# Last stage of an attention kernel: TensorE products on 64-column halves, and keys, queries and layer norm tokens transposed in pieces of 64 rows

## The reference

```
for l in range(2):                       # DEPTH
    h = shift_token(x)                   # second half of the features comes from the token before
    q, k, v = split(h @ wqkv[l])         # 8 heads of 64
    q = l2norm(q) * q_scale; k = l2norm(k) * k_scale
    q, k = rotary_xpos(q, k)
    o = local_attention(q, k, v)         # windows of 128 tokens, each sees itself and the one before
    x = x + o @ wo[l]
    h = layernorm(shift_token(x)) * ln_g + ln_b
    a, g = split(h @ w1[l] + b1[l])      # 682 hidden columns each
    x = x + (a * gelu(g)) @ w2[l] + b2[l]
```

## Time and profile before

| | |
|---|---|
| median of 3 runs | 2962.0 us (2961.99 to 2963.34) |
| span of the profiled execution | 2960.1 us |
| instructions on TensorE | 38016 matmuls, 38016 weight loads |
| TensorE, VectorE, ScalarE, GpSimd busy | 99%, 79%, 77%, 38% of the span |

### The profile page before, as it was taken

How to read it: one execution, slowest core, us unless ns; L and a number is a source line. 1 busy time by engine, 2 the same in 40 slices (tenths; PEclk the granted TensorE clock), 3 DMA queues, 4 the chain that set the end, 5 groups by cost and what they waited for, 6 DMA issues and landing times.

```text
span 2960.1 us, 97183 instructions
## 1 busy us (share of the span) xinstructions
PE 2919.8 (99%) x38016; PEld 1971.1 (67%) x38016; DVE 2325.1 (79%) x4219; ACT 2271.1 (77%) x4379; POOL 1111.0 (38%) x1835
## 2 busy tenths in 40 slices
PE   8999999999999999999989999999999999999998
PEld 4455555555555555555567777778777777877786
DVE  8888888888888888888856776667676667767665
ACT  4599999999999999999956666666666666666664
POOL 5421221111112211221245455555456554555554
PEclk9899999999999999999999999999999999999999
DMA  6631111111111111111121101111011111011110
GB/s 231 212 116 38 49 47 45 40 49 48 43 44 49 49 41 46 49 49 38 43 64 44 32 30 33 40 43 40 28 36 30 44 43 34 28 35 38 44 41 5
DMA packets 157206, 152.14 MB, mean 51 GB/s; under 512 B 17794, under 2 KB 130946, under 8 KB 156930
## 3 DMA queue, kind: packets, MB, share of 16 engines
q1 hardware_dynamic: 156930, 148.15, 16.0%
HBM read 89.37 MB, written 58.72 MB: 50 GB/s over the span
## 4 chain that ended last, share of the span: by engine, by line
PE 95%; DVE 3%; issue 1%; ACT 1%; SPq 0%; DMA 0%; POOL 0%; DVEq 0%; POOLq 0%; ACTq 0%
PE banks L1488 15%; PE banks L1450 15%; PE banks L1505 15%; PE banks L1690 11%; PE banks L1555 8%; PE banks L1703 6%; PE banks L1606 4%; PE banks L1645 4%; PE banks L1657 4%; PE banks L1566 4%; PE banks L1622 2%; PE banks L1578 1%; PE banks L1632 1%; PE banks L1587 1%; PE banks L1713 1%
## 5 line engine op out<-in xcount | busy, mean ns | idle before, releaser
L1146 DVE TENSOR_REDUCE pair_max<-banks 128x1 f32<-128x1024 f32 x1024 | 1219.7, 1222 | 145.5 <-PE banks L1450 115.8
L917 ACT ACTIVATE probs<-banks 128x512 f32<-128x512 f32 x2048 | 1158.7, 598 | 64.0 <-PE banks L1488 4.1
L1488 PE MATMUL banks<-q_aug,k_aug 98*32 98x512 bf16 x8192 | 1143.6, 381 | 0.8 <-ACT probs L917 0.4
L1450 PE MATMUL banks<-k_aug,q_aug 96*32 96x512 bf16 x8192 | 819.4, 382 | 5.3 <-ACT v_all L884 3.3
L1505 PE MATMUL banks<-probs,v_cur 128*32 128x256 f32 x8192 | 796.8, 379 | 0.2
L1488 PEld LDWEIGHTS banks<-q_aug,k_aug 98*32 98x32 bf16 x8192 | 391.7, 95 | 197.1 <-ACT probs L917 5.4
L1505 PEld LDWEIGHTS banks<-probs,v_cur 128*32 128x32 f32 x8192 | 366.8, 111 | 166.5 <-ACT acc_sb L898 0.8
L646 POOL TENSOR_SCALAR row_max<-pair_max 128x1 f32<-128x1 f32 x508 | 132.1, 283 | 886.5 <-DVE pair_max L1146 886.5
L1450 PEld LDWEIGHTS banks<-k_aug,q_aug 96*32 96x32 bf16 x8192 | 310.1, 97 | 218.2 <-DVE pair_max L1146 11.6
L1690 PEld LDWEIGHTS banks<-hnT,w_sb 128*128 128x128 f32 (+1 forms) x2816 | 320.2, 191 | 25.1 <-ACT hnT L997 25.1
L1690 PE MATMUL banks<-hnT,w_sb 128*128 128x128 f32 (+1 forms) x2816 | 332.4, 278 | 0.9 <-ACT hnT L997 0.9
(11 more groups left out here) (146 smaller groups left out, 4093.4 us busy)
## 6 DMA issues: line engine op xcount, KB each, us to landing
acc_scratch<-acc_sb SPq DMA_DIRECT2D x128, 256.0 KB, 2.4
heads_win<-acc_scratch SPq DMA_DIRECT2D x512, 64.0 KB
q_aug<-q_parts SPq DMA_DIRECT2D x192, 64.0 KB, 2.2
k_aug<-k_parts SPq DMA_DIRECT2D x192, 64.0 KB, 2.2
q_parts<-parts SPq DMA_DIRECT2D x16, 384.0 KB, 3.1
k_parts<-parts SPq DMA_DIRECT2D x16, 384.0 KB, 4.0
x_in<-in_x SPq DMA_DIRECT2D x10, 512.0 KB, 4.7
xT_scratch<-xnT SPq DMA_DIRECT2D x8, 512.0 KB, 5.2
```

Of the source, the lines that this page charges most:

```text
L917: nc.scalar.activation(probs[:, step % PRING, :], banks[:, ring(h, use), :], ACT.Exp, scale=SCALE).then_inc(prob_ready, 1)
L1146: nc.vector.tensor_reduce(pair_max[:, group % 2, q, half:half + 1], banks[:, 4 + 2 * (t % 2):6 + 2 * (t % 2), :], AX.XY, ALU.max).then_inc ...
L1450: last = nc.tensor.matmul(banks[m:m + CT, 4 + t % 4, :], q_aug[0:TERM_ROWS, b, q * P + m:q * P + m + CT], k_aug[0:TERM_ROWS, b, kq * BANK: ...
L1488: last = nc.tensor.matmul(banks[m:m + CT, ring(h, use), :], k_aug[0:AUG, b, kb * P + m:kb * P + m + CT], q_aug[0:AUG, b, qc * CHUNK:(qc + ...
```

## The change

Four things are changed, all in the last stage.

1. Products on halves. A helper `in_halves` issues each product as two, on columns 0 to 63 and 64 to 127 of its weights. It is used for the query projection (`project` with n = 0), the value projection, `project_o`, `hidden`, `project_hidden` and `project_heads`. The key projection (n = 1) stays whole, and so do L1632 (row sums) and L1722 (`transpose_y`).
2. Transposes in pieces. A helper `turn_rows` transposes rows 0 to 63 of a tile into bank 1 and rows 64 to 127 into bank 2. Keys and queries are transposed by it in one function, `transpose_qk`, with one semaphore `qkT_done`, and x1T by it in `transpose_h`. Keys lie in the first 256 columns of the two banks, queries in the last 256.
3. Readers follow. `keep_k`, `keep_q` and `normalise` read across two banks. `keep_k` waits for `qkT_done`, which comes after the queries too. The values go to bank 3 instead of bank 2, and the waits on `sum_ready` and `y_kept` are exchanged accordingly.
4. Two semaphores that no engine waits for, `turns_seen` and `x1_seen`, are incremented by TensorE after its waits on `k_turned`, `q_turned` and `x1_ready`.

```diff
+            def in_halves(out, stationary, moving, start, stop):
+
+                cols = stationary.shape[-1]
+                for first in range(0, cols, COLS):
+                    size = min(COLS, cols - first)
+                    last = nc.tensor.matmul(out[first:first + size], stationary[:, first:first + size], moving,
+                                            start=start, stop=stop)
+                return last
...
-                    last = nc.tensor.matmul(banks[:, lanes(b) + n, :], xT[:, l, b, f, 1 - f:1 - f + WINDOW],
-                                            wqkv_sb[:, l, f, n * INNER:(n + 1) * INNER],
-                                            start=(f == 0), stop=(f == 1))
+                    out, tokens = banks[:, lanes(b) + n, :], xT[:, l, b, f, 1 - f:1 - f + WINDOW]
+                    weights = wqkv_sb[:, l, f, n * INNER:(n + 1) * INNER]
+                    if n == 1:
+                        last = nc.tensor.matmul(out, tokens, weights, start=(f == 0), stop=(f == 1))
+                    else:
+                        last = in_halves(out, tokens, weights, start=(f == 0), stop=(f == 1))
...
+            def turn_rows(b, at_col, tile):
+
+                for r in range(2):
+                    rows = slice(r * LD, (r + 1) * LD)
+                    last = nc.tensor.transpose(banks[:, lanes(b) + 1 + r, at_col:at_col + LD],
+                                               tile[rows], ident[rows, rows])
+                return last
+
+            def transpose_qk(i, k):
 
                 l, b = parts_of(k)
                 if l == 0:
                     pe.wait_ge(y_kept, final_of(i, k) + (B * (k // ITEMS) + 1))
...
+                pe.wait_ge(k_turned, at(i, k))
+                nc.tensor.sem_inc(turns_seen, 1)
+                for j in range(NPAIR):
+                    turn_rows(b, j * LD, turned[:, b, 1, j * P:(j + 1) * P])
                 for j in range(NPAIR):
                     if j % 2 == 0:
                         pe.wait_ge(q_turned, at(i, k, j // 2 + 1, 2))
-                    last = nc.tensor.transpose(banks[:, lanes(b) + 3, j * P:(j + 1) * P],
-                                               turned[:, b, 0, j * P:(j + 1) * P], ident[:])
-                last.then_inc(qT_done, 1)
...
+                        nc.tensor.sem_inc(turns_seen, 1)
+                    last = turn_rows(b, D + j * LD, turned[:, b, 0, j * P:(j + 1) * P])
+                last.then_inc(qkT_done, 1)
...
                 pe.wait_ge(x1_ready, at(i, k))
+                nc.tensor.sem_inc(x1_seen, 1)
                 for f in range(2):
-                    last = nc.tensor.transpose(banks[:, lanes(b) + 3, f * P:(f + 1) * P],
-                                               x1T[:, l, b, f, 1 - f:1 - f + WINDOW], ident[:])
+                    last = turn_rows(b, f * LD, x1T[:, l, b, f, 1 - f:1 - f + WINDOW])
                 last.then_inc(h_done, 1)
...
-                        last = nc.tensor.matmul(
-                            banks[0:width, lanes(b) + bank, place_ * P:(place_ + 1) * P],
-                            w1_sb[:, l, f, c * P:c * P + width], hnT[:, b, f, :], start=(f == 0), stop=(f == 1))
+                        last = in_halves(banks[0:width, lanes(b) + bank, place_ * P:(place_ + 1) * P],
+                                         w1_sb[:, l, f, c * P:c * P + width], hnT[:, b, f, :],
+                                         start=(f == 0), stop=(f == 1))
```

More of the change, by code:

```diff
@@ L280, in build @@
         k_turned = sem("k_turned")
-        qT_done = sem("qT_done")
-        kT_done = sem("kT_done")
+        qkT_done = sem("qkT_done")
+        turns_seen = sem("turns_seen")
+        x1_seen = sem("x1_seen")
         qT_kept = sem("qT_kept")
@@ L1295, in normalise @@
                 b = k % B
-                h_tok = banks[:, lanes(b) + 3, 0:D]
+                h_tok = banks[:, lanes(b) + 1:lanes(b) + 3, 0:P]
                 dve.wait_ge(h_done, at(i, k))
@@ L1563, in project_v @@
                 if l == 0:
-                    pe.wait_ge(y_kept, final_of(i, k) + (B * (k // ITEMS) + 1))
+                    pe.wait_ge(sum_ready, final_of(i, k) + (B * (k // ITEMS) + 1))
                 for f in range(2):
-                    last = nc.tensor.matmul(banks[:, lanes(b) + 2, :], xT[:, l, b, f, 1 - f:1 - f + WINDOW],
-                                            wqkv_sb[:, l, f, 2 * INNER:], start=(f == 0), stop=(f == 1))
+                    last = in_halves(banks[:, lanes(b) + 3, :], xT[:, l, b, f, 1 - f:1 - f + WINDOW],
+                                     wqkv_sb[:, l, f, 2 * INNER:], start=(f == 0), stop=(f == 1))
                 last.then_inc(v_ready, 1)
-            def transpose_q(i, k):
+            def turn_rows(b, at_col, tile):
[5 more added lines that the diff above has]
+            def transpose_qk(i, k):
                 l, b = parts_of(k)
                 if l == 0:
-                    pe.wait_ge(sum_ready, final_of(i, k) + (B * (k // ITEMS) + 1))
+                    pe.wait_ge(y_kept, final_of(i, k) + (B * (k // ITEMS) + 1))
+                pe.wait_ge(k_turned, at(i, k))
+                nc.tensor.sem_inc(turns_seen, 1)
+                for j in range(NPAIR):
+                    turn_rows(b, j * LD, turned[:, b, 1, j * P:(j + 1) * P])
                 for j in range(NPAIR):
@@ L1656, in project_o @@
                     for j in range(NPAIR):
-                        last = nc.tensor.matmul(banks[:, lanes(b) + 1, f * P:(f + 1) * P],
-                                                wo_sb[:, l, j, f * P:(f + 1) * P], oT[:, b, j, :],
-                                                start=(j == 0), stop=(j == NPAIR - 1))
+                        last = in_halves(banks[:, lanes(b) + 1, f * P:(f + 1) * P],
+                                         wo_sb[:, l, j, f * P:(f + 1) * P], oT[:, b, j, :],
+                                         start=(j == 0), stop=(j == NPAIR - 1))
                 last.then_inc(wo_done, 1)
@@ L1702, in project_hidden @@
                     for f in range(2):
-                        last = nc.tensor.matmul(banks[:, lanes(b), f * P:(f + 1) * P],
-                                                w2_sb[:, l, j, f * P:(f + 1) * P], uT[:, b, j, :],
-                                                start=(j == 0 and f == 0), stop=(j == HB - 1 and f == 1))
+                        last = in_halves(banks[:, lanes(b), f * P:(f + 1) * P],
+                                         w2_sb[:, l, j, f * P:(f + 1) * P], uT[:, b, j, :],
+                                         start=(j == 0 and f == 0), stop=(j == HB - 1 and f == 1))
                 last.then_inc(w2_done, 1)
@@ L1712, in project_heads @@
                 for f in range(2):
-                    last = nc.tensor.matmul(banks[:, lanes(b) + 3, 0:D], heads_T[:, b, f, :], wp_sb[:, f, :],
-                                            start=(f == 0), stop=(f == 1))
+                    last = in_halves(banks[:, lanes(b) + 3, 0:D], heads_T[:, b, f, :], wp_sb[:, f, :],
+                                     start=(f == 0), stop=(f == 1))
                 last.then_inc(proj_done, 1)
```

34 lines of the change are left out of this document (15 added, 19 removed).

## The result

The changed kernel takes 3021.65 us (median of 4 runs, 3017.29 to 3027.91), the kernel before 2961.99 beside it: ratio 1.0203, 95% interval 1.0188 to 1.0217. It is 60 us slower; the forecast was 2949 and its range ended at 2963. The profiled execution took 3017.29 us with a span of 3015.5.

A forecast was written before the change was run, and what follows sets the result against it. TensorE was taken as busy 99% of the span, with waits at x1T, hnT and the exponentials. Passes gaining 0.24 (final), 0.20 and 0.14 us gave 13.1 us over 16 windows: 2949 us; own range 2943 to 2955, 8 in 10: 2934 to 2963.

The forecast's parts named there:

- Part 1: Query projection: the change of shape ahead and the slow first weight load go, -0.20 us a pass; VectorE's chain follows.
- Part 2: project_o, keys and queries: savings lie beside VectorE's chain to x1T, so nothing reaches the end.
- VectorE's shadow: From query projection to x1T, VectorE's chain lasts 2.48 us whatever TensorE does, hiding TensorE's savings there.
- Part 3: x1T to the scores: wait +0.07, pieces and change of shape -0.02, value projection's first pair +0.05; sum +0.10 us.
- B's double price: Changes between column and row halves cost twice 0.09: +0.18 us in x1T to scores, 2961 us; chance 0.18.
- Part 4: hidden: 5.01 us to 4.85 on halves, -0.16, or -0.15 unrounded; start bound to keep_normed.
- C's mechanism: Pairs of halves sharing a streamed operand and bank run slower than 0.109 us, making the kernel slower; chance 0.14.
- Part 5: project_hidden: 2.70 us to 2.62 on halves, -0.08 us.
- Part 6: Final passes: y transposed whole behind halves needs one more change of shape, +0.09 us; heads stay at 0.86.
- the 17th load: Second half of L1622: in passes that aren't final it starts 0.12 us behind the exponentials, letting through 0.10 and 0.04.
- Rival A: Waits on x1T and the exponentials don't bind: 28 us more gained, 2921 us; chance 0.13 together with its milder form.
- its milder form: Changes between column and row halves are free: 12 us more gained, 2937 us; chance 0.13 together with Rival A.

The follow-up runs named there:

- e1: The changed kernel with TensorE's loop of the last stage written out in full: 2952.71 us, ratio 0.9969 to the kernel before.
- e8: The kernel before with query projection, hidden and project_hidden on halves and TensorE's last-stage loop written out: 2949.36 us, ratio 0.9960.
- e10: As e8, with keys and queries also transposed in 64-row pieces, plus their readers, exchanged waits and turns_seen increments: 2948.86 us, ratio 0.9954.
- e11: The changed kernel with TensorE's loop written out and without the increment of x1_seen: 2947.22 us, ratio 0.9950 to the kernel before.
- e2: The kernel before with TensorE's loop of the last stage written out in full: 2960.68 us, ratio 0.9999.
- e13: The kernel before with 24 increments of an unread semaphore in each pass inside hidden, loop kept: 3069.68 us, ratio 1.0366.
- e9: The kernel before with query projection on halves, keys and queries in 64-row pieces with their readers, waits and turns_seen, loop kept: 3007.77 us, ratio 1.0143.
- e6: The kernel before with only hidden on halves, loop kept: 3009.96 us, ratio 1.0160.
- e12: The kernel before with query projection and project_hidden on halves, loop kept: 3018.69 us, ratio 1.0192.

## Why the prediction was wrong

The forecast's mechanism was right where it looked, and the sum lacked a term larger than all others. **The step that failed** is in the change part by part: it says that a pair of halves does the work of one whole instruction, and costs the pair at its pace of 0.109 us. It counted twice as many instructions only by their time on the array. That they are also code, in a loop that had stayed on the chip with 1640 instructions, stood in no step and no rival. TensorE's instruction counts and the queue of instructions without a row during the loop were there to be read. In place of nothing this cost 64.7 us, the difference of the profiled executions of after and e1. Without it the forecast would have held: e1's 2952.71 lies in its own range of 2943 to 2955.

The parts by what e1 and the pass above measured:

- Part 1, query projection, forecast -0.20: 1840.78 - 1837.27 = 3.51 in place of 3.71, -0.20. VectorE followed; its wait is below 0.1, as said.
- Part 2, nothing: the time agrees (e8 to e10 0.5 us). But whole transposes would not have stayed in VectorE's shadow behind the faster query projection: x1T's start 0.16 behind the sum in e8. The pieces win 0.08 of that back, and what follows loses most of it.
- Part 3, forecast +0.10: x1T starts 0.14 behind the sum (0.05 before), +0.09 for the forecast's +0.07; from x1T to the scores 2.14 in place of 2.09, +0.05 for +0.03. Together +0.14. The change from row to column halves costs 0.09 at most. For the one from column to row halves, the last pair of the value projection and the scores start 0.52 apart in e1, as the last whole instruction and the scores did before: 0.09 above the pace of 0.43. So B's double price fell.
- Part 4, forecast -0.15: `hidden` 1852.77 - 1847.92 = 4.85, as forecast to 0.01. A pair is 0.109, so C's mechanism fell; slower came by another road.
- Part 5, forecast -0.08: 1855.42 - 1852.77 = 2.65, -0.05.
- Part 6, forecast +0.09: heads to y 0.97 in place of 0.86, +0.11.

The sum for a final pass is -0.20 + 0.14 - 0.16 - 0.05 + 0.11 = -0.16 for the forecast -0.24. In e1 the four passes take 21.83, 23.15, 22.97 and 21.71 us (medians; before 21.97, 23.13, 23.13, 21.96), -0.53 a turn for the forecast -0.82. What a pass that isn't final gains past the exponentials is given back at the 17th load, and shows in the length of the one behind it (23.15). In e1 that load stands 0.11 behind the exponentials (0.17 and 0.23 before), as forecast. In e11, without `x1_seen`, a turn is 0.85 shorter than before and the time is 2947. So the mis-sized term of the small ones was mainly part 3.

Rival A (no shadow) fell: e1 is 9 us faster than the kernel before, where A had 41 and its milder form 25.

## What to carry to other kernels

Before splitting instructions inside a hardware loop, count each engine's instructions in the body, and look whether the instruction queue is silent while the loop runs: if it is, growth of the body can turn that off at once, here with about 3 us and often a half clock at each jump back. A body near the limit can tip by its length or by code ahead of it; time it again after either. Writing out the 15 turns of this loop took the gaps away at no cost in time (e1, e2), and it shows what an edit is worth by itself.

## What the runs showed of the hardware

- A body of 1672 instructions on TensorE stayed, one of 1736 was fetched at two of 14 jumps (e13), one of 1748 in every turn (e9); one of 1640 stayed at shifts of 0, 64 and 256 instructions and was fetched at three of 14 jumps at 128.
- At a jump back to code that isn't held, the matmuls on either side start 2.4 to 4.6 us apart, and the clock is at 0.5 behind many such gaps (7 of 14 in e6, 9 in e12, 10 in after, 13 in e9).
- Written out, 2450 instructions in 89.66 us stream at no cost in time (e1).
- 24 increments in a row on TensorE between products cost 1.7 us (0.07 each, e13); one between a wait and the instruction that it guards costs 0.09 (e1 and e11).
- A change from column to row halves costs 0.09 us (e1), as one to or from whole.
